# Pair products by quads of fields, with GpSimd adding the feature halves of 8 rounds

## What is computed

```python
e = jnp.stack([tbl_0[ids[:, 0]], ..., tbl_31[ids[:, 31]]], axis=1)   # 2048 x 32 x 64
pw = jnp.einsum('bpi,pij->bpj', e[:, ids_x, :], w)
z = jnp.einsum('bpj,bpj->bp', pw, e[:, ids_y, :])                    # 496 pairs
h = jnp.concatenate([z, dense_ctx], axis=1)
h = jnp.maximum(h @ W_top1 + b_top1, 0.0)      # 512 x 512
h = jnp.maximum(h @ W_top2 + b_top2, 0.0)      # 512 x 256
y = h @ W_top3                                 # 256 x 1
```

## Time and profile before

| | us |
|---|---|
| runs: lowest, median, highest of 3 | 1136.27, 1137.32, 1141.85 |
| the profiled execution | 1127.72 |
| its span, first to last instruction | 1125.9 |
| PE matmul busy | 899.1 |
| DVE busy | 597.6 |
| POOL busy | 483.4 |
| ACT busy | 67.6 |

### The profile page before, as it was taken

The page is one execution under the profiler, slowest core; times in us unless marked ns, Lnnn a source line. Parts: engine busy times, 40 slices in busy tenths (PEclk is TensorE's granted clock), DMA queues, the critical chain, the costliest instruction groups (busy, mean ns, idle before and its releaser), DMA issues.

```text
span 1125.9 us, 11138 instructions
## 1 busy us (share of the span) xinstructions
PE 899.1 (80%) x4592; PEld 308.5 (27%) x4592; DVE 597.6 (53%) x512; ACT 67.6 (6%) x109; POOL 483.4 (43%) x516
## 2 busy tenths in 40 slices
PE   0320259999967789999997599999996599999999
PEld 0100013333322223333332133333332133333333
DVE  0100037778734445667774345567863355578880
ACT  0000000000000000000000000000000000100001
POOL 6777546543266625435356625435356632000000
PEclk9985669999987889999998889999998889999999
DMA  9311101100011101000011101000011100000000
GB/s 325 97 27 26 21 15 24 20 17 13 10 20 22 23 11 19 15 15 18 12 19 23 23 10 20 16 14 19 12 19 24 23 9 11 1 1 1 1 1 0
DMA packets 19348, 28.05 MB, mean 25 GB/s; under 512 B 8913, under 2 KB 9681, under 8 KB 18513
## 3 DMA queue, kind: packets, MB, share of 16 engines
q0 software_dynamic: 16384, 16.81, 8.1%
q1 hardware_dynamic: 2914, 10.53, 2.6%
HBM read 27.30 MB, written 0.01 MB: 24 GB/s over the span
## 4 chain that ended last, share of the span: by engine, by line
PE 70%; another core or an unknown queue 19%; DVE 5%; issue 3%; ACT 1%; DMA 1%; POOL 1%; DVEq 0%; POOLq 0%
PE main_ps L240 37%; PE z_ps L254 21%; PE x_ps L287 6%; DVE prod L312 5%; PE x_ps L223 3%; PE main_ps L287 2%; PE main_ps L241 2%; ACT e_t L323 1%; POOL emb L187 1%; DMA emb<-in_tbl,idx 1%; PE z_ps L258 0%; DMA idx<-in_ids 0%; DVEq L114 0%; ACT ctx_y L342 0%
## 5 line engine op out<-in xcount | busy, mean ns | idle before, releaser
L312 DVE TENSOR_TENSOR prod<-main_ps,e_t 128x1024 f32<-128x1024 f32 x512 | 597.6, 1218 | 500.3 <-PE main_ps L241 258.3
L187 POOL DMA_INDIRECT emb<-in_tbl,idx x512 | 483.2, 944 | 453.5 <-PE x_ps L223 244.4
L240 PE MATMUL main_ps<-e_t,w_sb 64*128 64x512 f32 x1024 | 512.3, 632 | 189.8 <-DVE prod L312 83.2
L241 PE MATMUL main_ps<-e_t,w_sb 64*128 64x512 f32 x1024 | 512.4, 632 | 0.0
L240 PEld LDWEIGHTS main_ps<-e_t,w_sb 64*128 64x128 f32 x1024 | 181.4, 192 | 465.8 <-issue 258.0
L254 PE MATMUL z_ps<-prod,const_sb 128*32 128x512 f32 x2048 | 264.9, 638 | 0.3 <-DVE prod L312 0.3
L241 PEld LDWEIGHTS main_ps<-e_t,w_sb 64*128 64x128 f32 x1024 | 181.1, 192 | 0.0
L254 PEld LDWEIGHTS z_ps<-prod,const_sb 128*32 128x32 f32 x2048 | 55.7, 114 | 192.8 <-issue 136.4
L323 ACT ACTIVATE e_t<-x_ps 128x512 f32<-128x512 f32 x64 | 38.2, 597 | 681.7 <-PE x_ps L223 341.5
L223 PE MATMUL x_ps<-const_sb,emb 128*128 128x128 f32 x256 | 44.5, 299 | 34.3 <-DMA emb<-in_tbl,idx 31.7
L223 PEld LDWEIGHTS x_ps<-const_sb,emb 128*128 128x128 f32 x256 | 28.6, 148 | 89.8 <-issue 75.0
(11 more groups left out here) (10 smaller groups left out, 11.8 us busy)
## 6 DMA issues: line engine op xcount, KB each, us to landing
emb<-in_tbl,idx POOLq DMA_INDIRECT x512
w_sb<-in_w SPq DMA_DIRECT2D x5, 1280.0 KB
w_sb<-in_w SPq DMA_DIRECT2D x1, 1024.0 KB
w_sb<-in_w SPq DMA_DIRECT2D x1, 512.0 KB
w_sb<-in_w SPq DMA_DIRECT2D x1, 448.0 KB
w_sb<-in_w SPq DMA_DIRECT2D x1, 384.0 KB
w_sb<-in_w SPq DMA_DIRECT2D x1, 320.0 KB
w_sb<-in_w SPq DMA_DIRECT2D x1, 256.0 KB, 3.4
```

The lines of the kernel that those rows point to most:

```text
L187: pool.indirect_dma_start(out=emb[:, n % G_SLOTS, s, odd * EMBED:(odd + 1) * EMBED], out_offset=None, in_=tables[f], in_offset=bass.Indire ...
L240: nc.tensor.matmul(main_ps[:, slot, :], w_sb[LOW, u, :], even[LOW, 0, :], start=True, stop=True)
L241: nc.tensor.matmul(main_ps[:, slot + 1, :], w_sb[UP, u, :], odd[UP, 0, :], start=True, stop=True)\
L312: nc.vector.tensor_tensor(prod[:, s:s + 2, :], main_ps[:, slot:slot + 2, :], e_q, ALU.mult)\
```

## The change

Two duos form a **quad** (4 fields). A "low" unit pairs duo m with the low 32 features of the four fields of a quad, a "high" unit with the high 32; both have the same four pairs of fields per row half, so their products can be added before the reduction. Pairs inside what a quad can't cover are "duo" and "twin" units. There are 128 units a tile as before, in 32 rounds of two pieces: both firsts, then both seconds. ScalarE writes, for every duo above 1, four more copies of 32 partitions from x_ps into quad_t, ahead of the copy that signals.

GpSimd adds the high products of a round onto the low ones (128x2048, in place) in rounds 2, 7, 11, 14, 18, 22, 26 and 29 of each tile; those reductions have 4 matmuls. In its program the additions stand among the gathers, which are dealt out over the rounds. DVE_FOLDS is empty, so what the diff has for it never runs. Reductions trail by two rounds (PAST = 2), prod holds 12 units, the gather ring 6 duos, e_t 6, quad_t 8 quads. The context matmuls are gone: SyncE writes the 16 context rows into z_sb, and each tile's result goes out by itself.

The core of the diff:

```diff
+def order_pieces():
+    pieces = []
+    for m in range(DUOS - 1, 1, -1):
+        if m % 2 == 0:
+            pieces.append(("duo", m, m + 1))
+        pieces += [("low", m, q) for q in range(QUADS - 1, m // 2, -1)]
+    pieces.insert(len(pieces) - 2, ("duo", 0, 1))
+    return pieces + [("low", m, q) for q in range(QUADS - 1, 0, -1) for m in (1, 0)]
+
+
+SECOND = {"duo": "twin", "low": "high"}
+PIECES = order_pieces()
+ROUND = 4
+ROUNDS = 2 * len(PIECES) // ROUND
+UNITS = []
+for _r in range(ROUNDS):
+    _two = PIECES[2 * _r:2 * _r + 2]
+    UNITS += _two + [(SECOND[_k], _a, _b) for _k, _a, _b in _two]
 NUNIT = len(UNITS)
-FIRST_OF_DUO = [min(u for u, mq in enumerate(UNITS) if m in mq or (mq[0] == mq[1] == m - 1)) for m in range(DUOS)]
-FINAL_OF_DUO = [max(u for u, mq in enumerate(UNITS) if m in mq or (mq[0] == mq[1] == m - 1)) for m in range(DUOS)]
-ROUND = 4
-ROUNDS = NUNIT // ROUND
+
+
+def duos_of(u):
+    kind, m, q = UNITS[u]
+    return (m, q) if kind in ("duo", "twin") else (m, 2 * q, 2 * q + 1)
+
+
+def moved_of(u):
+    kind, m, q = UNITS[u]
+    return (m, q) if kind in ("duo", "twin") else (m,)
+
+
+FIRST_OF_DUO = [min(u for u in range(NUNIT) if m in duos_of(u)) for m in range(DUOS)]
+FINAL_OF_DUO = [max(u for u in range(NUNIT) if m in moved_of(u)) for m in range(DUOS)]
+FINAL_OF_QUAD = [max((u for u, (k, _, q) in enumerate(UNITS) if k == "high" and q == Q), default=-1) for Q in range(QUADS)]
...
-P_SLOTS = 8
+P_SLOTS = 12
+PAST = 2
 LAG = 4
-E_SLOTS = 24
-G_SLOTS = 8
-
-
-def z_row(u, x, upper):
-    kt, c = divmod(2 * u + x, 64)
-    s, g = divmod(c, 4)
-    return kt * P + 32 * g + 2 * s + upper
+E_SLOTS = 6
+Q_SLOTS = 8
+G_SLOTS = 6
+FULL = [r for r in range(ROUNDS) if all(PIECES[2 * r + h][0] == "low" for h in range(2))]
+DVE_FOLDS, POOL_FOLDS = [], FULL[::3]
+POOL_GATHERS = 5
...
-DUO_ROUNDS = (-4, -3, -2, -1, 0, 1, 2, 5, 7, 9, 11, 13, 16, 19, 22, 25)
-MLP_ROUNDS = (3, 4, 6, 8, 10, 12, 14)
+W1_ROWS = w1_rows()
+CTX_ROWS = [[(z % P, W1_ROWS[z] - PAIRS) for z in range(kt * P, kt * P + P) if W1_ROWS[z] >= PAIRS] for kt in range(KTILES)]
+
+DUO_ROUNDS = (-4, -3, -2, -1, 0, 1, 2, 4, 6, 8, 10, 13, 16, 19, 21, 22)
+MLP_ROUNDS = (3, 5, 7, 9, 11, 12, 14)
...
-                r = t * ROUNDS + u // ROUND - 1
+                r = t * ROUNDS + u // ROUND - PAST
...
+            def gather(n, k):
+                t, m = n // DUOS, DUOS - 1 - n % DUOS
+                if n == DUOS and k == 0:
                     pool.wait_ge(idx_in[1], 16)
                     pool.nop(nofuse=True)
-                for m in range(DUOS - 1, -1, -1):
-                    n = duo_number(t, m)
-                    if n >= G_SLOTS:
-                        pool.wait_ge(transposed, n - G_SLOTS + 1)
-                        pool.nop(nofuse=True)
-                    for odd in range(2):
-                        f = 2 * m + odd
-                        for s in range(SUBS):
-                            pool.indirect_dma_start(
-                                out=emb[:, n % G_SLOTS, s, odd * EMBED:(odd + 1) * EMBED], out_offset=None,
-                                in_=tables[f], in_offset=bass.IndirectOffsetOnAxis(
-                                    ap=idx[:, t, f * SUBS + s:f * SUBS + s + 1], axis=0),
-                            ).then_inc(gathered[n % G_SLOTS], 16)
-
+                if n >= G_SLOTS and k == 0:
+                    pool.wait_ge(transposed, n - G_SLOTS + 1)
+                    pool.nop(nofuse=True)
+                odd, s = divmod(k, SUBS)
+                f = 2 * m + odd
+                pool.indirect_dma_start(
+                    out=emb[:, n % G_SLOTS, s, odd * EMBED:(odd + 1) * EMBED], out_offset=None,
+                    in_=tables[f], in_offset=bass.IndirectOffsetOnAxis(
+                        ap=idx[:, t, f * SUBS + s:f * SUBS + s + 1], axis=0),
+                ).then_inc(gathered[n % G_SLOTS], 16)
+
+            def fold(t, r):
+                s = 2 * ((NUNIT * t + ROUND * r) % P_SLOTS)
+
+                pool.wait_ge(products, NUNIT * t + ROUND * (r + 1))
+                pool.nop(nofuse=True)
+                low, high = prod[:, s:s + ROUND, :], prod[:, s + ROUND:s + 2 * ROUND, :]
+                nc.gpsimd.tensor_tensor(low, low, high, ALU.add).then_inc(pool_folded, 1)
+
+            todo = [(n, k) for n in range(TILES * DUOS) for k in range(2 * SUBS)]
+            seen = G_SLOTS
+            for kind, t, n in EVENTS:
+                if kind == "duo":
+                    seen = duo_number(t, n) + 1 + G_SLOTS
+                elif kind == "unit" and n % ROUND == ROUND - 1:
+                    room = len([g for g in todo if g[0] < seen])
+                    for _ in range(min(room, POOL_GATHERS if t or n > 10 * ROUND else room)):
+                        gather(*todo.pop(0))
+                    if n // ROUND in POOL_FOLDS:
+                        fold(t, n // ROUND)
...
+            for t in range(TILES):
+                for kt in range(KTILES):
+                    if CTX_ROWS[kt]:
+
+                        sp.wait_ge(z_out, KTILES * t + kt + 1)
+                    for row, f in CTX_ROWS[kt]:
+                        sp.dma_start(z_sb[row:row + 1, kt, :], ctx_t[f:f + 1, t * TILE:(t + 1) * TILE]).then_inc(ctx_in, 16)
+                if t > 0:
+                    sp.wait_ge(evicted, EVICTED["mlp", t - 1, MLP_STEPS - 1])
+                    sp.dma_start(out[:, (t - 1) * TILE:t * TILE], y_sb[:, :]).then_inc(y_out, 16)
...
-                if r == ROUNDS - 1 and t == 0:
-                    pe.wait_ge(ctx_in, 16)
-                for k in range(2 * ROUND):
-                    c = 2 * ROUND * (r % ROUNDS_KT) + k
-                    s, g = divmod(c, 4)
-                    last = nc.tensor.matmul(z_ps[32 * g:32 * g + 32, :], sel[:, 30 - 2 * s:62 - 2 * s],
-                                            prod[:, (2 * (NUNIT * t + ROUND * r) + k) % (2 * P_SLOTS), :], start=(s == 0), stop=(s == 15 and r < ROUNDS - 1))
-                if r == ROUNDS - 1:
-                    for g in range(4):
-                        last = nc.tensor.matmul(z_ps[32 * g:32 * g + 32, :], ctx_sel[:, g, :],
-                                                ctx_sb[:, t * TILE:(t + 1) * TILE], start=False, stop=True)
+                if r in DVE_FOLDS:
+                    pe.wait_ge(folded, len(DVE_FOLDS) * t + DVE_FOLDS.index(r) + 1)
+                if r in POOL_FOLDS:
+                    pe.wait_ge(pool_folded, len(POOL_FOLDS) * t + POOL_FOLDS.index(r) + 1)
+                rr = r % ROUNDS_KT
+                for p in range(2 if r in DVE_FOLDS or r in POOL_FOLDS else ROUND):
+                    kind, slot = UNITS[ROUND * r + p][0], 2 * ((NUNIT * t + ROUND * r + p) % P_SLOTS)
+                    for x in range(2):
+                        g = 2 * (p % 2) + x
+                        if kind in ("low", "high"):
+                            lhs = sel_quad[:, 28 - 4 * rr:60 - 4 * rr]
+                        else:
+                            s = 2 * rr + (kind == "twin")
+                            lhs = sel_duo[:, 30 - 2 * s:62 - 2 * s]
+                        last = nc.tensor.matmul(z_ps[32 * g:32 * g + 32, :], lhs, prod[:, slot + x, :], start=(rr == 0 and p < 2),
+                                                stop=(rr == ROUNDS_KT - 1 and p >= 2 - 2 * (r in DVE_FOLDS or r in POOL_FOLDS)))
                 last.then_inc(reduced, 1)
...
-                    e_q = e_duo(t, m + 1, 2) if m == q else e_duo(t, q).to_broadcast([P, 2, TILE])
+                    if kind == "twin":
+                        e_q = e_duo(t, q, 2)
+                    elif kind == "duo":
+                        e_q = e_duo(t, q).to_broadcast([P, 2, TILE])
+                    else:
+                        h = int(kind == "high")
+                        e_q = quad_t[:, quad_slot(t, q), h:h + 1, :].to_broadcast([P, 2, TILE])
...
+                q = m // 2
+                if q > 0:
+                    gone, r = divmod((QUADS - 1) * t + QUADS - 1 - q - Q_SLOTS, QUADS - 1)
+                    if gone >= 0 and m % 2:
+
+                        act.wait_ge(products, NUNIT * gone + FINAL_OF_QUAD[QUADS - 1 - r] + 1)
+                    for h in range(2):
+                        for x in range(2):
+                            rows, to = EMBED * x + HALF * h, EMBED * (m % 2) + BLOCK * x
+                            nc.scalar.activation(quad_t[to:to + BLOCK, quad_slot(t, q), h, :], x_ps[rows:rows + HALF, :], ACT.Copy)
                 nc.scalar.activation(e_duo(t, m)[:, 0, :], x_ps[:, :], ACT.Copy).then_inc(evicted, 1)
```

More of the change, by code:

```diff
@@ L154, in dlrm_tower @@
         products = sem("products")
+        folded = sem("folded")
+        pool_folded = sem("pool_folded")
         reduced = sem("reduced")
@@ L313, in _ @@
                       .then_inc(products, 1)
+                    if u % ROUND == 1 and n >= ROUND and (u // ROUND - 1) % ROUNDS in DVE_FOLDS:
+                        dve.wait_ge(products, n - 1)
```

(38 more changed lines are left out.)

64 lines of the change are left out of this document (33 added, 31 removed).

## The result

| | before | changed |
|---|---|---|
| median of 4 runs each | 1138.43 us (1136.27 to 1141.85) | 1232.54 us (1226.12 to 1239.46) |
| ratio, 95% interval | | 1.0825 (1.0759 to 1.0890) |
| profiled execution: span, mean granted clock | 1125.9 us, 0.924 | 1237.7 us, 0.866 |

The changed kernel is 8.25% slower. The forecast had the side right and the size wrong: +34 us were forecast, +94 came in the medians, +111.8 in the two profiled spans. The time lies above the range.

A forecast was written before the change was run, and what follows sets the result against it. TensorE was taken as the bound, held up by late completions during GpSimd's gather bursts. Boundaries +66.9, start -2, folds -27.2 and context matmuls -3.4 gave +34 us, taking the median from 1137.3 to 1171; range 1098 to 1205.

The forecast's parts named there:

- The law of 1.40 us per gather: In unbroken GpSimd gather bursts, TensorE's completions are held until 1.40 us per gather after the start; 16 gathers lose 10.9 us.
- The middles: Rounds from a tile's first to third K tile: no burst loss charged, only the folds' gain of 0.85 us a round.
- The recorded sign of being wrong: Prediction is wrong if 25 gathers hold no completions, or pace away from boundaries changes by more than the folds.
- The boundaries, +66.9: Between tiles, bursts of 10, 25, 25 and 20 gathers lose 61.6 us each, against 44.3, 36.8 and 36.8 before.
- The clock: At each boundary, 3.0 us left over beyond the burst law, mostly put down to slow clock behind a stall.
- The folds, -27.2: 32 folded rounds each save TensorE one reduction wave, 0.85 us; a folded round lasts 4.64 us instead of 5.49.
- The start of tile 0, -2: First burst ends after 80 gathers; a lead of 20 us less evictions 4.5, late folds 2.6 and a burst 10.9.
- The addition, 4.8 us: GpSimd's 128x2048 addition, taken as two serial reads, 4.8 us, between bounds of 2.4 and 7.2.
- Rival C: GpSimd's additions are slow, 7.2 us each, adding some 10 us: 1181; chance 0.55 together with the main forecast.
- Rival B: GpSimd additions and VectorE products block each other on memory: +134 us, less the gains 1235; chance 0.07.
- Rival A: Additions or their waits break gather streams early, so bursts cost no more than now: 1105 or 1087; chance 0.26.
- D: Bursts broken at 16 to 20 gathers: half the extra, +33 us, cancels the gains: 1137; chance 0.12.

The follow-up runs named there:

- b_pace: The kernel before the change, with a small GpSimd memset and a wait for it after every gather: 1075.38 us, 5.1% faster than the kernel before.
- a_stop: The changed kernel with GpSimd's waits for the products kept but no additions, all reductions of 8 matmuls: 1188.37 us.
- a_nofold: The changed kernel with neither additions nor their waits, all reductions of 8 matmuls: 1134.57 us, against 1133.11 for the kernel before.
- the first four experiments: b_pace, a_pace, a_stop and a_nofold, run where completions were held back; the kernel before took 1133.11 us beside them.
- a_skip0: The changed kernel without the additions of tile 0, where nothing is held: 887.93 us against 904.58 for the kernel before, ratio 0.9806.
- a_pace: The changed kernel with a small GpSimd memset and a wait for it after every gather: 1239.42 us.

## Why the prediction was right in its side and wrong in its size

Of the 78 us that the forecast lacks in the profiled spans, counted to the end of each boundary's last stall, the middles have 34, the boundaries 29 and the start of tile 0 has 18, and the end takes back 5.

- **The law of 1.40 us per gather: right.** It gives the next gather at 115.5 us after the first burst; it came at 116.68, a first burst of 80 gathers as forecast. It gives the ends of the stalls in the bursts of 25 and 15 within half a microsecond. b_pace, one run on one chip, shows that the unbroken gathers are the cause and not only go with it.
- **The middles: the step that failed.** The sum had a term for each boundary and none for bursts in the rounds between, where it gave only the folds' gain: 106.0 less four folded rounds, 4 x 0.85, is 102.6 us. I followed GpSimd's order gather by gather at the boundaries, and here only took over that the ring breaks bursts at 8. It does not: bursts of 15 and 16 came in two middles. Without the end of the stall in front of them these took 120.8 and 120.9 us, some 18 above forecast each; the law gives 9.5 for a burst of 15 and 10.9 for one of 16, in sum 20.4. The last middle has no such burst and took 95.4, where 97.7 was forecast. The recorded sign of being wrong, a pace away from the boundaries that changes by more than the folds, is what came. Beside a_stop's middle of 107.3 us the 134.8 of the changed kernel are 24.2 us more idle time, 13.0 of it before TensorE's first unit, and 3.3 more busy time: 34 records fewer, at 100.82 / 544 = 0.185 us each, save 6.3, and the lower clock costs the other 9.6.
- **The boundaries, +66.9: right in mechanism, too small in size.** The bursts came as listed: 10, 25, 25, 20. A boundary was forecast at 167 us, and 162 to 163 lie between the marks, but that this looks near is luck of where the mark falls: with the last 14.0 us of the stall it took 176 to 177, some 10 more each. In the boundary from 608.70 TensorE is idle for 58.2 us up to there (44.2 between the marks and 14.0 behind), against 25.8 before: 32 more, where 24.8 were forecast in all. The waits alone, without what the folds save, cost 66.5 us at the boundaries beside a_nofold, and 55.8 beside the profiled kernel before (501.1 - 445.3).
- **The clock: mis-sized.** I took 3.0 us per boundary for slow clock behind stalls. The mean granted clock fell from 0.924 to 0.866, and the 27.2 + 3.4 us of removed matmuls turned up as 10.2 us less busy time: by this estimate some 20 us were lost to the clock.
- **The folds, -27.2: right where TensorE is free.** A folded round lasts 4.63 us, as forecast 4.64 (1127.73 to 1132.36 below).

```profile
1127.73 1.06 PE L328 MATMUL z_ps<-prod,const_sb 128*32 128x512 f32 x8
1132.36 1.92 PE L328 MATMUL z_ps<-prod,const_sb 128*32 128x512 f32 x16
1137.85 1.92 PE L328 MATMUL z_ps<-prod,const_sb 128*32 128x512 f32 x16
```

- **The start of tile 0, -2: wrong by 18.** To the third K tile, with the six folds ahead of it (-5.1), -7.1 was forecast, and +10.9 came. By estimate one round, 5.5 us, of it is that reductions trail a round more, which I had not charged to this mark, and which comes back at the end (part of -7.8). The rest stays open.
- **The addition, 4.8 us: 4.53.** The Trainium skill, GPSIMD Engine Reference, section 3.1, has 4497 ns for it; the trace agrees, with 4531 ns. **Rival C**, 7.2 us, falls.
- **Rival B**, additions and products blocking each other, falls (M with it): the product takes 1.219 us in the changed kernel and 1.219 in a_nofold, and beside the addition of 558.59 TensorE's matmuls start 0.43 us apart (559.14, 559.57, 560.00), as before. By the rule of the Trainium skill, SBUF — State Buffer, "two separate sides", on VectorE instructions with two SBUF inputs, it could not happen, since these products have one; the trace agrees. That the result lies near B's 1235 us is chance, and its terms add up to 1239.
- **Rival A**, the additions break the stream, and **D**, the bursts broken at 16 to 20, fall by GpSimd's timeline: bursts of 25.
- **What no case had:** Q, the addition late by its place in GpSimd's order. It costs 44 us where nothing is held and 0.2 in the comparison. I had charged it 2.6 us (folds 7 and 14), since I reckoned that TensorE would be held anyway.

**Still open:** why the chip of the first four experiments holds completions and four others do not; whether the density of the gathers or the lack of any pause of some length starts it; what makes the stalls of the boundaries longer with additions; and whether a_skip0 is faster on a chip that holds. For the last there is no measurement, and the waits at the boundaries, which cost 66 us there, are still in it.

## What to carry to other kernels

Work put on an engine in between its DMA issues changes the pattern of these issues: follow that engine's program order through every stage, and ask of each pause that now breaks a run of gathers whether it survives a shift by the new instruction's length. An operation that another engine waits for is as late as all that stands ahead of it in its engine's order, so leave it out where that engine starts with a long backlog. A mark taken from one engine can fall inside another's stall: look at what stands on both sides of it before a loss is given to a stage. And one comparison can hang on a cost that other chips don't have: the change is +8.3% where completions are held and +3.0% where not, and a small variant of it -1.9%.

## What the runs showed of the hardware

- In the comparison and on the chip of the first four experiments, and not on four other chips, TensorE's completions came late while GpSimd issued indirect DMAs every 1.25 us: in the long first burst VectorE's products start 11.2 us or twice that apart, in a burst of 25 there is a gap of 20.5 us (410.62 to 431.10), and the pile has arrived 1.40 us per gather after the burst's start. The same kernel takes 1133 to 1138 us with it and 904 to 905 without. A pause that adds 0.64 us after each gather ends it (b_pace, a_pace).
- That pause, a memset of 128x64 and a wait for it, is 0.17 us of work and 0.77 of idle time around it before the next gather (0.30 without it).
- In the changed kernel's stall from 103.8 to 116.7 us TensorE was idle throughout, and was granted 0.50 of its clock, the level of 1.2 GHz:

```profile
103.80:116.70 12.90, 0.00 (x0) 0.00 (x0) 2.74 (x3) 0.74 (x2) 0.02 (x1) 0.50 0.01 3
```
